# Query projections of a cross-attention by seven block products instead of eight

## The reference

```python
h = layer_norm(x, ln1)                       # then ln2 for the second attention
qh = (h @ wq + bq)                           # 512 -> 16 heads x 128
kh = (ctx @ wk + bk)                         # ctx: the 128 context rows of each sequence
vh = (ctx @ wv + bv)                         # one bias row is joined to kh and to vh
weights = softmax(qh @ kh.T / sqrt(128))
x = x + (weights @ vh) @ wo + bo
...                                          # the same with the second set of weights
x = x + gelu(layer_norm(x) @ w_fc1 + b_fc1) @ w_fc2 + b_fc2
```

## Time and profile before

| | us |
|---|---|
| median of 3 runs (2986.56 to 2992.95) | 2988.18 |
| the profiled execution | 2985.3 |
| its span | 2983.5 |

### The profile page before, as it was taken

The page is one execution under the profiler, slowest core; times in us unless marked ns, Lnnn a source line. Parts: engine busy times, 40 slices in busy tenths (PEclk is TensorE's granted clock), DMA queues, the critical chain, the costliest instruction groups (busy, mean ns, idle before and its releaser), DMA issues.

```text
span 2983.5 us, 40485 instructions
## 1 busy us (share of the span) xinstructions
PE 2823.4 (95%) x14352; PEld 2118.4 (71%) x14352; DVE 1902.5 (64%) x2743; ACT 1099.0 (37%) x2409; POOL 535.6 (18%) x373
## 2 busy tenths in 40 slices
PE   5989898997989999999999999999999999999899
PEld 2333333333778888888888878788888888888687
DVE  5989989897866555556555474565555655555644
ACT  3232323322534333334333343343343433433432
POOL 2857657473001000000000010010000000000100
PEclk8999899998999999999999999999999999999999
DMA  4010010111143222222222211132222222222111
GB/s 164 1 30 29 16 42 0 58 43 43 61 155 124 82 72 94 80 92 82 82 87 77 96 67 63 43 113 81 98 81 82 84 75 98 81 84 75 53 49 56
DMA packets 140224, 215.64 MB, mean 72 GB/s; under 512 B 10033, under 2 KB 76593, under 8 KB 139025
## 3 DMA queue, kind: packets, MB, share of 16 engines
q1 hardware_dynamic: 137264, 210.70, 20.3%
q0 software_dynamic: 2880, 3.94, 0.7%
HBM read 164.53 MB, written 46.14 MB: 71 GB/s over the span
## 4 chain that ended last, share of the span: by engine, by line
PE 64%; DVE 4%; DMA 1%; ACT 1%; issue 1%; DVEq 0%; ACTq 0%; SPq 0%
PE ca_ps L60 19%; PE ca_ps L62 19%; PE ca_ps L61 19%; PE ca_ps L1991 4%; PE ca_ps L1981 4%; DVE ca_stats L68 1%; DMA xres<-pb_dram 1%; PE ca_ps L2018 1%; DVE ca_pb L1745 1%; DMA pb_dram<-ca_pb 0%; ACT ca_pr L1552 0%; DVE ca_pr L1741 0%; DVE ca_mx L1733 0%; DVE ca_ctx_lo L1786 0%; DVE raw L1755 0%
## 5 line engine op out<-in xcount | busy, mean ns | idle before, releaser
L1552 ACT ACTIVATE ca_pr<-ca_ps,ca_nb 128x129 f32<-128x129 f32 x512 | 181.8, 368 | 487.8 <-DVE ca_nb L1735 487.7
L60 PE MATMUL ca_ps<-ca_h_hi,ca_wq_hi 128*128 128x512 f32 x768 | 313.2, 408 | 4.4 <-DVE ca_h_lo L1780 3.9
L617 DVE TENSOR_TENSOR_SCAN tm_xn<-tm_wd,tm_vb 128x512 f32<-128x512 f32 x256 | 298.5, 1208 | 12.7
L1505 POOL TENSOR_TENSOR ca_dv<-ca_bvr 128x256 f32<-128x256 f32 x32 | 23.6, 739 | 1563.7 <-DVE xq L1720 1404.5
L62 PE MATMUL ca_ps<-ca_h_hi,ca_wq_lo 128*128 128x512 f32 x768 | 302.8, 394 | 0.0
L61 PE MATMUL ca_ps<-ca_h_lo,ca_wq_hi 128*128 128x512 f32 x768 | 301.6, 393 | 0.0
L60 PE MATMUL ca_ps<-ca_wv_hi,ca_ctx_hi 128*128 128x256 f32 x1024 | 296.2, 289 | 2.1 <-DVE ca_wv_lo L1715 2.1
L62 PE MATMUL ca_ps<-ca_wv_hi,ca_ctx_lo 128*128 128x256 f32 x1024 | 286.7, 280 | 0.0
L61 PE MATMUL ca_ps<-ca_wv_lo,ca_ctx_hi 128*128 128x256 f32 x1024 | 286.6, 280 | 0.0
L60 PE MATMUL ca_ps<-ca_wo_hi,ca_ct_hi 128*128 128x512 f32 x640 | 256.0, 400 | 1.0 <-DVE ca_ct_lo L1749 0.8
L61 PE MATMUL ca_ps<-ca_wo_lo,ca_ct_hi 128*128 128x512 f32 x640 | 252.7, 395 | 0.0
(11 more groups left out here) (232 smaller groups left out, 5966.5 us busy)
## 6 DMA issues: line engine op xcount, KB each, us to landing
pb_dram<-ca_pb SPq DMA_DIRECT2D x128, 256.0 KB, 2.0
xres<-pb_dram SPq DMA_DIRECT2D x128, 256.0 KB, 2.7
ca_sq<-in_wq SPq DMA_DIRECT2D x49, 512.0 KB, 5.9
ca_so<-in_wo SPq DMA_DIRECT2D x48, 512.0 KB, 3.8
ca_sk<-in_wk SPq DMA_DIRECT2D x33, 512.0 KB, 6.9
ca_sv<-in_wv SPq DMA_DIRECT2D x32, 512.0 KB, 4.0
x_dram<-xres SPq DMA_DIRECT2D x8, 1024.0 KB, 4.2
ca_bvr<-in_bvb SPq DMA_DIRECT2D x32, 256.0 KB, 5.3
```

Of the source, the lines that this page charges most:

```text
L60: pe.matmul(out, lhs[0], rhs[0], start=first, stop=False)
L617: v.tensor_tensor_scan(state[t % 2][:, d, :], wd[:, g].rearrange("p b t -> p (b t)"), pair[:, d, :], 0.0, ALU.mult, ALU.add).then_inc(scan ...
L1552: ins = act.activation(pr[hd][:, b, :], ps[:, BANK_SC + b // 2, o:o + KW], ACT.Exp, bias=nbs[hd][:, b:b + 1], scale=SCALE, accum_out=sms[h ...
```

## The change

From the second pair of heads on (`g` = 1 to 7) the two queries of a unit are no longer two products of 128 x 512 x 512, but one product of 256 x 512 x 512 in 2 x 2 blocks by the Strassen and Winograd scheme: seven block products of 128 x 256 x 256 where eight would be needed. One block product is 6 matmuls with 256 columns. It needs four sums of weight blocks for each pair of heads (POOL, `weight_sums` and `weight_sum_in_place`), four sums of blocks of the normed rows for each quad and stage (POOL, `row_sums` and `row_sum_in_place`, with the low halves on POOL too, `rows_lo`), high halves of these on ACT, low halves of the weight sums on DVE, and seven additions of 256 columns on DVE for each unit to put the results together (`fast_last_quarter`, `fast_other_quarters`). The first product goes to SBUF by ACT (`p1_out`). The first pair of heads and the MLP use the plain products.

Some things are moved to make room: one `pr` and one `pb` tile in place of two, tiles laid over others, `bo` loaded for one stage at a time, the second half's context loaded later, and several semaphores joined into one. The core of the diff:

```diff
@@ def units
-            with engine.Fori(1, G) as g:
+            with engine.Fori(1, G - 1) as g:
                 slot(Unit(h, st, g - 1, 1), Unit(h, st, g, 0))
                 slot(Unit(h, st, g, 0), Unit(h, st, g, 1))
+            slot(Unit(h, st, G - 2, 1), Unit(h, st, G - 1, 0))
+            slot(Unit(h, st, G - 1, 0), Unit(h, st, G - 1, 1))
@@ tensor: slot
                 scores(A, 0)
-                query(C, 0, BANK_Q)
                 key(C, 0)
                 scores(A, 1)
-                query(C, 1, BANK_Q)
+                pe.wait_ge(o_out, A.o * 4)
+                fast(C, Q_BANKS)
                 key(C, 1)
-                value(C, 0, A.o * 4 - 1)
+                pe.wait_ge(q_out, C.n * 2 + 2)
+                value(C, 0, A.o * 4)
@@ tensor: new
+            def product(out, a, b):
+                for c in range(2):
+                    ins = mm3(pe, out, [t[:, c, :] for t in a], [t[:, c, :] for t in b], c == 0, c == 1)
+                return ins
...
+                product(out[0], a11, b11).then_inc(fast_full, 1)
+                product(out[1], s2, t2).then_inc(fast_full, 1)
+                product(out[2], s3, t3).then_inc(fast_full, 1)
+                product(out[3], s1, t1).then_inc(fast_full, 1)
+                product(out[4], a12, b21).then_inc(fast_full, 1)
+                pe.wait_ge(p1_read, C.fast + 1)
+                product(out[0], a22, minus_t4).then_inc(fast_full, 1)
+                pe.wait_ge(fast_sum, C.sums + 1)
+                product(out[1], s4, b22).then_inc(fast_full, 1)
@@ tensor: scores
-                pe.wait_ge(q_out, A.n * 2 + (hd + 1))
+                pe.wait_ge(q_out, A.n * 2 + 2)
@@ vector: new
+            def fast_u(C, p1, banks):
+                w = C.fast
+                v.wait_ge(p1_read, w + 1)
+                v.wait_ge(fast_full, w * 7 + 2)
+                v.tensor_tensor(x1[:], p1, ps[:, banks[1], 0:HALF], ALU.add).then_inc(fast_sum, 1)
+                v.wait_ge(fast_full, w * 7 + 3)
+                v.wait_ge(fast_sum, C.sums + 1)
+                v.tensor_tensor(u3[:], x1[:], ps[:, banks[2], 0:HALF], ALU.add).then_inc(fast_sum, 1)
+                v.wait_ge(fast_full, w * 7 + 4)
...
+            def fast_other_quarters(C):
+                v.wait_ge(fast_full, C.fast * 7 + 5)
+                quarter(C, 0, qT[0][:, 0:HALF], Q_BANKS[4], qT[0][:, 0:HALF]).then_inc(q_out, 1)
...
+                quarter(C, 0, qT[0][:, HALF:QT], Q_BANKS[1], x1[:]).then_inc(q_out, 1)
@@ vector: slot
                 row_max(A, 0)
                 normalise(A, 0)
+                key_col(C, 0)
                 row_max(A, 1)
+                fast_last_quarter(C)
+                normalise(A, 1)
                 if C.quad == 0:
-                    key_col(C, 0)
                     split_one(wv, sv, wv_hi, wv_split, C.wkv)
                 else:
                     split_one(wo, so, wo_hi, wo_split, C.wq)
-                normalise(A, 1)
+                fast_other_quarters(C)
@@ scalar: second
+                rows_hi(A)
+                row_in_place_hi(A)
                 split_one(wk, sk, wk_in, wk_hi, C.wkv + 1)
                 context_hi(A, 0)
                 context_hi(A, 1)
                 norm_hi(C.ln, C.st, 1)
+                weight_sums_hi(N)
+                rows_hi(C)
                 query_out(C, 0, BANK_Q)
                 split_q(C.wq + 1, 0)
                 query_out(C, 1, BANK_K)
-                split_q(C.wq + 1, 1)
+                split_q_fast(C.wq + 1)
+                weight_sum_in_place_hi(N)
+                row_in_place_hi(C)
@@ gpsimd: new
+                add_bo(h, st, 0)
+                row_sums(unit(0, 0))
+                used(unit(0, 0))
+                row_sum_in_place(unit(0, 0))
+                rows_lo(unit(0, 0))
+                row_lo_in_place(unit(0, 0))
+                add_bo(h, st, 1)
...
+                weight_sums(unit(1, 0))
+                row_sums(unit(0, 1))
+                rows_lo(unit(0, 1))
+                used(unit(0, 1))
+                weight_sum_in_place()
+                row_sum_in_place(unit(0, 1))
+                row_lo_in_place(unit(0, 1))
```

More of the change, by code:

```diff
@@ L1294, in cross_attend @@
     TB = 32
+    HALF = QT // 2
+    Q_BANKS = (0, 2, 3, 4, 7)
     LN_BANKS = (0, 1, 5, 6)
@@ L1372, in __init__ @@
                 self.ln = (h * 3 + st) * 2 + quad
+                self.stage = h * 2 + st
+                self.fast = g * 2 + (quad - 2 + 14 * self.stage)
+                self.sums = self.fast * 5
+                self.plain = 4 * self.stage + 2 * quad + 32 * h
+                self.ws = g + (7 * self.stage - 1)
         class MlpUnit:
@@ L1462, in _ @@
                     more = h == 0 or i < 15
-                    if h == 0 and i == 1:
-                        for quad in range(2):
-                            sp.wait_ge(c_split, quad + 1)
-                            ctx_in(1, quad)
+                    if i % 8 == 1:
+                        next_bo(h, i // 8)
                     if i > 0:
@@ L1480, in _ @@
                     sp.dma_start(so[:], io["wo"][i + 1]).then_inc(wo_in, 16)
+                    if h == 0 and i == 15:
+                        sp.wait_ge(fast_full, 7 * 28)
+                        for quad in range(2):
+                            ctx_in(1, quad)
                 probs(h, 15, 1)
@@ L1486, in _ @@
                     q = h * 24 + i
+                    if i == 17 and h == 0:
+                        next_bo(h, 2)
                     if h == 0 and i == 18:
@@ L1527, in _ @@
+            value_bias(0)
+            stage(0, 0, range(1, 9))
+            stage(0, 1, range(9, 17))
+            add_bo(0, 2, 0)
+            add_bo(0, 2, 1)
+            stage(1, 0, range(17, 25))
+            stage(1, 1, range(25, 32))
+            add_bo(1, 2, 0)
+            add_bo(1, 2, 1)
         @block.scalar
@@ L1622, in slot @@
                 key_out(C, 0)
+                p1_out(C, qT[0][:, 0:HALF], Q_BANKS[0])
                 exps(A, 1)
-                query_out(C, 1, BANK_Q)
                 if C.quad == 1:
+                    act.wait_ge(fast_full, C.fast * 7 + 7)
                     split_q(C.wq + 1, 0)
+                    if more_sums(C):
+                        split_q_fast(C.wq + 1)
+                    else:
+                        split_q(C.wq + 1, 1)
                 key_out(C, 1)
-                if C.quad == 1:
-                    split_q(C.wq + 1, 1)
+                if C.quad == 1 and more_sums(C):
+                    N = Unit(C.h, C.st, C.g + 1, 0)
+                    weight_sums_hi(N)
+                    weight_sum_in_place_hi(N)
                 context_hi(A, 0)
```

271 lines of the change are left out of this document (207 added, 64 removed).

## The result

| kernel | median us | ratio to before, 95% interval |
|---|---|---|
| before (4 runs beside the change) | 2987.55 | |
| the change (4 runs, 3041.58 to 3053.35) | 3047.43 | 1.0197 (1.0172 to 1.0221) |

A forecast was written before the change was run, and what follows sets the result against it. PE was taken to bound the slots, never waiting in them. -36 (matmuls) + 35 (slot waits) + 43 (edges) = +42 us, 2985.3 to 3027.3; the median, 2.9 above, forecast as 3030 us; 3003 to 3056 holds 8 in 10.

The forecast's parts named there:

- Saved on PE: In each of 56 slots: two queries at 5.50 us become a fast product at 4.85, saving 0.65, 36 us in all.
- The scores of head 1 "at nothing": In a slot: exponentials of head 0 and PE are ready together, scores start near 3.7 us, no added cost.
- The wait at the values: In slots: PE waits for DVE's last quarter, 28 x 0.5 + 28 x 0.75 = 35 us.
- the 0.25 us for POOL's weight sums in every second slot: In every second slot: POOL's weight sums meet DVE's weight split, charged a third of a POOL add.
- The openings: At stage edges: 0.9 + 0.5 + 5.0 + 3.9 = 10.3 us per stage, 41 for four, plus 2 for a context product.
- 5.0 of new wait: At the end of `second`: PE may begin scores of head 0 at 1376.3 in place of 1371.3, behind POOL's row sums.
- The turns: Behind `turn`: scores wait for both queries, 1.1 us added and 0.2 of key wait gone, +0.9.
- POOL not slowed at the edges: Rival, chance 0.18: at stage edges POOL does not slow down, edges cost 22 us, kernel +21, 3009 us.
- DVE is later than laid out: Rival, chance 0.14: DVE's 17-instruction chain runs 0.35 us later per slot, 20 us, a few more at edges: 3055 us.
- The last quarter in time: Rival, chance 0.12: cheaper additions remove the slots' wait but 28 x 0.25; 2981 us with edges of 22.
- Its condition: For that rival: faster only if the wait in a slot and the edges together cost less than 36 us.

The follow-up runs named there:

- the three moves: Against the changed kernel: output weights split behind the quarters, bias adds last in POOL's list, value weights split ahead in first-quad slots; 2994.37 us (1.0037).
- the one that gives PE more work: Against the changed kernel: 24 plain matmuls with 512 columns in place of the fast product's 42 with 256; 3047.46 us (1.0215).
- two experiments: Bias adds last in POOL's list, against the changed kernel, 3033.32 us; POOL's row sums behind DVE's splits, against the three moves, 2998.85 us.
- three orders of it: The three moves, 2994.37 us; on these, POOL's row sums behind DVE's splits, 2998.85; on that, ACT's query copies ahead of its high halves, 2996.46.
- the last kernel: Against the kernel before: fast product only from the third pair of heads, row sums in plain slots, splits moved, own-query wait; 2969.28 us (0.9941).
- the experiment with the queries' copies first: Against the kernel with row sums behind DVE's splits: ACT copies both plain queries out before the row sums' high halves; 2996.46 us (1.0031).

## Why the prediction was right or wrong

- **Saved on PE**: laid out 0.65 us a slot, 36 in all. Measured 24 x 0.229 = 5.50 for the queries and 42 x 0.118 = 4.94 for the fast product: 0.56, 31 us. I had taken the fast product's cost from one run of values, 0.114 each, and allowed only 1% on it. Matmuls of the same width are not equally far apart everywhere: with the three moves the 24 values take 2.75 us, 0.114 each, while the fast product in the same slots keeps its 5.04, 0.118 each and 0.1 behind the scores. Why is open.
- **The scores of head 1 "at nothing"**: right to 0.1. They come 3.68 us behind those of head 0 (3.66 to 3.7 laid out), but they take 0.88 us in place of 0.81 to the next matmul: 56 x 0.07 = 4 us, where I had charged nothing.
- **The wait at the values**: 35 us laid out. A typical wait is 0.61 us in the second quad's slots and 0.71 in the first's; over the 52 slots of the table the key with the wait takes 0.62 more than before on average, 35 us in 56. DVE's chain was right to 0.35 us over 17 instructions (12.91 for 12.57). That DVE's last quarter holds it is shown by the experiments that take the split away and the one that gives PE more work. Wrong was the 0.25 us for POOL's weight sums in every second slot. There the split took its 1.19 us and POOL was stretched, since DVE had issued first, and the wait in these slots is the shorter one. So the right total is partly luck: it came out of 0.2 too little in the first quad's slots and 0.14 too much in the second's.
- **The openings**: 41 us with the small steps laid out, and 2 more for a late context. Measured 22.1 (`second`) + 17.8 - 0.9 (first slots, less what every slot has) + 3.4 (`turn`) = 42.4. POOL's list from the first low half to the last row sum was laid out as 20.6 us and took 20.63. Within it the stretching is larger in the bias adds (6.00 for 4.97) and the weight sums (3.7 for 2.4) than I had put there, but the sum holds. Counted from the start of `second`, the scores of head 0 were to come 5.5 us later (5.0 of new wait and 0.5 for splits) and came 5.85 later; of these only 3.8 is the new wait for ACT, and 2.1 lie ahead of it, in the contexts, transposes and outputs that DVE serves late (the section on what was not expected shows by what). The turns lost 1.7 us each where 0.9 was laid out. The scores of head 1 were laid out 7.6 us behind those of head 0 and are 7.31 to 7.40. That the sum comes out right is luck in part: some 3 of the 42 us are PE's lower clock (see the same section), for which nothing was charged.
- **Not in the sum at all**: 3.6 us from the first half's end to the second's opening, and 4.5 us where the values take 2.88 us on average in place of 2.80, since they start slower behind a wait. With the 5 us of the first point and the 4 of the second these are 17 us; between +42 and the +58 that the change's own parts show lie 16.
- **The rivals**: POOL not slowed at the edges is refuted by the changed kernel's own rows (its bias adds take 6.00 us for 4.97, its weight sums 3.7 for 2.4), and by DVE's splits of 2.25 and 0.68 us in two experiments. "DVE is later than laid out" had its 0.35 us, but not its 20: PE came 0.15 us later as well, and the wait grew by 0.1 in this slot. "The last quarter in time" is refuted for this kernel, and is what the three moves made true. Its condition (edges and waits under 36 us together) was right in kind, but a fast slot without a wait saves 0.5 us and not 0.65, so the limit is 28 us: with the waits gone and the edges at some 32 us the kernel was still 9 us slower than before, and with the edges reduced as well it was faster.

What I had not seen is which of the two costs a better order can remove. The slots' wait goes with two moved splits. The edges' chain does not go by moving its parts: three orders of it gave 2994, 2999 and 2996 us, with intervals that overlap. What helped was to give it more time.

## What to carry to other kernels

Saved matmuls count only where PE is what the stretch waits for afterwards too: lay out the other engine's chain between the same two points, and compare the slack with the saving before anything is built. Work that prepares such a saving once for each stage belongs where the stage has time; doing the first units in the old way gave up 8 x 0.5 = 4 us of saving, and the openings with the turns, 42 us longer with the change and 32 with the three moves, were 6 us longer in the last kernel. And where two engines block each other, moving one's work out of a queue can put it beside the other's: look at the durations of both in the new place, of DVE's instructions with one SBUF input too.

## What the runs showed that was not expected

The prediction counted only DVE's instructions with two SBUF inputs as held up by POOL. The largest delay is in one with a single SBUF input, the scaling of the normed rows in `second`. These are its four pieces before, with the change, and with the fast product from the third pair on:

```profile
1351.49 1.92 DVE L1768 TENSOR_SCALAR raw<-raw,ca_mv,ca_rstd 128x512 f32<-128x512 f32 x4
1375.91 4.92 DVE L1975 TENSOR_SCALAR raw<-raw,ca_mv,ca_rstd 128x512 f32<-128x512 f32 x4
1349.64 1.92 DVE L2008 TENSOR_SCALAR raw<-raw,ca_mv,ca_rstd 128x512 f32<-128x512 f32 x4
```

A piece takes 0.54 us alone. Beside POOL's low halves, whose first was issued at 1376.76, the third piece (1376.83) takes 2.60 and the fourth 1.48; in the last kernel POOL does nothing at that time. It is so in all four `second`. Behind these 3.0 us DVE makes the low half of the contexts, which now starts 19.2 us after the start of `second` (1383.57) and not 16.3 (1356.36), and PE's output product stands idle 1.1 us for it.

PE's clock falls after the new waits, and the first slot pays for it. After the idle 3.68 us ahead of the scores at 962.28, the changed kernel's trace shows the key's matmuls with 512 columns 0.43 us apart in place of 0.23, the lower of the clock's two levels (1.2 GHz for 2.4):

```profile
963.79 0.63 PE L61 MATMUL ca_ps<-ca_ctx_lo,ca_wk_hi 128*128 128x512 f32 x1
964.22 0.63 PE L62 MATMUL ca_ps<-ca_ctx_hi,ca_wk_lo 128*128 128x512 f32 x1
```

```profile
962.00:969.70 7.70, 5.49 (x21) 4.32 (x21) 5.02 (x6) 4.34 (x14) 5.23 (x5) 0.78 0.01 3
969.70:976.00 6.30, 6.30 (x40) 6.30 (x41) 4.04 (x10) 3.15 (x11) 0.00 (x0) 0.73 0.26 82
```

In the first stretch this costs nothing, since the exponentials are later still. In the second, behind another idle 1.93 us, it does: in the two stages where the clock is low there too (0.73 and 0.76), the first slot takes 31.4 and 31.3 us, against 29.8 in the two where it is not (29.85 and 29.77). That is 1.5 us each time, about 3 of the openings' 42. In the experiment with the queries' copies first, PE is idle 3.5 us ahead of the scores of head 1, and the slower stretch comes in all four stages.
